# Attention turned by a product, 16-bit integer quantising, and GpSimd on two of eight blocks

## What is computed

```python
# attention, per head: s_mat = scores * d_mat (decay, causal)
h = (s_mat @ v) / (max(abs(sum(s_mat)), exp(-m)) + 5e-5)
h = h * rsqrt(mean(h * h) + 1e-6) * (1 + outnorm_w)
x = x + tanh(g_xattn[0]) * h
# feed-forward: xq = clip(round(x / scale) + zp, -128, 127), scale and zp from min and max of all x
h = gelu(((xq(x) - zx) @ wq(W1).T) * (sx * sw) + b1)          # 128 -> 512
x = x + tanh(g_ffn[0]) * (((xq(h) - zh) @ wq(W2).T) * (sh * sw2) + b2)
```

## Time and profile before

| | |
|---|---|
| median of 3 runs | 905.29 us (905.22 to 906.47) |
| profiled execution: own time | 905.67 us |
| its span | 903.9 us |
| busy: TensorE, VectorE, ScalarE, GpSimd | 617.6, 676.0, 430.6, 196.3 us |
| chain that ended last | TensorE 55%, VectorE 33%, issue 5%, ScalarE 5% |

### The profile page before, as it was taken

How to read it: one execution, slowest core, us unless ns; L and a number is a source line. 1 busy time by engine, 2 the same in 40 slices (tenths; PEclk the granted TensorE clock), 3 DMA queues, 4 the chain that set the end, 5 groups by cost and what they waited for, 6 DMA issues and landing times.

```text
span 903.9 us, 16672 instructions
## 1 busy us (share of the span) xinstructions
PE 617.6 (68%) x5953; PEld 437.7 (48%) x6037; DVE 676.0 (75%) x1896; ACT 430.6 (48%) x892; POOL 196.3 (22%) x160
## 2 busy tenths in 40 slices
PE   4957999923425830000170479999999999999998
PEld 3943444411124630000160376777666777777776
DVE  6658467788979659899799875655666778878775
ACT  2425455457762363333560436556554445445543
POOL 3000168611436002221000036777000000000000
PEclk9999999975555985555585758999999999999999
DMA  7000000000001000000040000000000000001000
GB/s 195 24 1 0 2 1 1 2 1 1 1 14 33 1 1 1 9 12 12 14 140 0 1 1 1 2 2 1 1 2 13 2 13 0 12 0 35 0 13 13
DMA packets 20747, 13.12 MB, mean 15 GB/s; under 512 B 1580, under 2 KB 19240, under 8 KB 20680
## 3 DMA queue, kind: packets, MB, share of 16 engines
q1 hardware_dynamic: 20680, 12.27, 4.9%
HBM read 9.12 MB, written 2.10 MB: 12 GB/s over the span
## 4 chain that ended last, share of the span: by engine, by line
PE 55%; DVE 33%; issue 5%; ACT 5%; SPq 1%; DMA 1%; DVEq 0%; POOL 0%; ACTq 0%; POOLq 0%
PE PS L1494 7%; PE PS L1509 6%; PE PS L1511 6%; PE PS L1510 6%; PE PS L1495 6%; DVE Bm L1078 5%; DVE rowm L1090 5%; PE PS L1493 5%; DVE A L1073 4%; PE PS L1268 2%; PE PS L1334 2%; DVE hmm L1015 2%; DVE hmm L1016 2%; DVE A L728 2%; PE PS L1344 2%
## 5 line engine op out<-in xcount | busy, mean ns | idle before, releaser
L691 ACT ACTIVATE A<-PS,small_t 128x512 f32<-128x512 f32 x256 | 168.4, 688 | 123.9 <-PE PS L1495 122.4
L1509 PE MATMUL PS<-kT_w,A 128*128 128x128 bf16 x1024 | 174.8, 219 | 0.0
L1510 PE MATMUL PS<-kT_w,A 128*128 128x128 bf16 x1024 | 174.8, 219 | 0.0
L1511 PE MATMUL PS<-kT_w,A 128*128 128x128 bf16 x1024 | 174.7, 219 | 0.0
L1184 DVE TENSOR_TENSOR A<-A 128x512 bf16<-128x512 f32 x192 | 123.5, 690 | 12.0 <-ACT A L691 10.8
L1446 PE MATMUL PS<-identf,slab 128*128 128x128 f32 x128 | 21.1, 321 | 125.2 <-ACT xn_w L658 121.8
L1509 PEld LDWEIGHTS PS<-kT_w,A 128*128 128x128 bf16 x1024 | 100.2, 98 | 11.3 <-issue 4.6
L1510 PEld LDWEIGHTS PS<-kT_w,A 128*128 128x128 bf16 x1024 | 100.2, 98 | 6.6
L1494 PE MATMUL PS<-A,xn_w 128*128 128x512 bf16 (+1 forms) x256 | 98.2, 384 | 3.6 <-issue 0.4
L1511 PEld LDWEIGHTS PS<-kT_w,A 128*128 128x128 bf16 x1024 | 100.2, 98 | 0.0
L1495 PE MATMUL PS<-A,xn_w 128*128 128x512 bf16 (+1 forms) x256 | 98.3, 384 | 0.0
(11 more groups left out here) (287 smaller groups left out, 1279.1 us busy)
## 6 DMA issues: line engine op xcount, KB each, us to landing
slab<-in_L_ffn_w_dram SPq DMA_DIRECT2D x16, 256.0 KB, 3.1
xs<-in_x_dram SPq DMA_DIRECT2D x4, 512.0 KB, 6.3
cs<-in_ctx_dram SPq DMA_DIRECT2D x4, 512.0 KB, 6.8
out_dram<-xs SPq DMA_DIRECT2D x8, 256.0 KB, 2.3
A<-Bm SPq DMA_DIRECT2D x9, 64.0 KB, 2.0
xn_w<-in_L_ffn_W_dram SPq DMA_DIRECT2D x2, 256.0 KB, 2.9
A<-Bm SPq DMA_DIRECT2D x4, 36.0 KB, 1.8
A<-Bm SPq DMA_DIRECT2D x4, 24.0 KB, 1.8
```

Of the source, the lines that this page charges most:

```text
L691: act.activation(hf[:, e % 2, c, :], bank(c), ACT.Gelu_apprx_tanh, bias=b1).then_inc(S["h_gelu"], 1)
L1509: pe.matmul(o, hh[:, e % 2, c, t], w2h[:, e, c, :], start=(c == 0 and k == 0), stop=False, skip_group_check=True)
L1510: pe.matmul(o, hh[:, e % 2, c, t], w2l[:, e, c, :], start=False, stop=False, skip_group_check=True)
L1511: ins = pe.matmul(o, hl[:, e % 2, c, t], w2h[:, e, c, :], start=False, stop=(c == NC - 1), skip_group_check=True)
```

## The change

- `turn` is a real f32 product with a constant `tmat` (68 columns of the identity and 64 columns of identity times gain, per half: 132 columns) in place of the transpose. `keep` copies 264 columns, and the gain product of GpSimd (L424) and of `late_norm` (L964) is gone. `tmat` is made on GpSimd once the gain is there, and TensorE waits for it (`turn_made`) ahead of the loop. `oall` is a ring of 16 blocks.
- ScalarE's `keep(b - 2)` stands behind `keep_turned(b - 1)`; `squares`, `divisors` and `mean_squares` come one block earlier; `turn(30)` stands ahead of `weigh(31)`; `ln_stats(1, 0)` is done at block 24. Behind the loop VectorE's order is now `x_range(5, 0)`, `late_norm(6)`, `ln_scales(1, 0)`, `divisors(7)`, `x_range(5, 1)`, `mean_squares(7)`, `x_stats(6)`, `late_norm(7)`, `x_stats(7)`, `x_range(6, 0)`, `ln_stats(1, 1)`, `x_range(6, 1)`, `x_range(7, 0)`, `x_range(7, 1)`.
- Quantising: ScalarE writes int16 with no constant added, VectorE clips int16 to bf16, GpSimd's step is gone. The first 512 columns of x are scaled and clipped by VectorE alone (`xq_first`). The load of the gelu table is asked for ahead of the scaling (`gwarm`).
- Second layer: ScalarE scales six blocks, GpSimd blocks 2 and 5 (`HPOOL`); the clip of nb stands ahead of `add2(nb - 2)` and `x3_stats(nb - 3)`.
- The product of b2 with its gate moves from behind `affine` to ahead of the attention loop.

```diff
+XCUTS = [(512, 1024), (1024, 2048), (2048, 3072), (3072, 4096)]
+HPOOL = [2, 5]
...
-        oall = Bm[:, 4352:8704].rearrange("p (b w) -> p b w", b=B)
+        oall = Bm[:, 4352:8576].rearrange("p (n w) -> p n w", n=16)
+        tmat = Bm[:, 10240:10504].rearrange("p (s c) -> p s c", s=2)
...
+        hqi = Bm[:, 0:8192].bitcast(I16).rearrange("p (c t) -> p c t", c=NC)
+        xqi = Bm[:, 8192:10240].bitcast(I16)
...
+        gwarm = mm[:, 23:24]
...
+            ident4 = identf[:].rearrange("p (j w) -> p j w", j=4)
+            for half in range(2):
+                pool.tensor_copy(tmat[:, half, 0:4 * VW].rearrange("p (j w) -> p j w", j=4), ident4[:, :, 0:VW])
...
             pool.wait_ge(S["gain_ready"], 1)
+            for half in range(2):
+                ins = pool.tensor_tensor(tmat[:, half, 4 * VW:4 * VW + 4 * DH].rearrange("p (j w) -> p j w", j=4), ident4[:, :, 0:DH],
+                                         onw_b[:, 64 * half:64 * half + 64].rearrange("p (j w) -> p j w", j=4), ALU.mult)
+            ins.then_inc(S["turn_made"], 1)
+            pool.wait_ge(S["turn_made"], 1)
...
             def normed(m):
-                chain(pool.tensor_tensor(t.rearrange("p (m w) -> p m w", w=DH), heads(m)[:, :, 0:DH], last(f, DH), ALU.mult), m, 3)
+                chain(pool.tensor_tensor(by_head(osq[:, m % 2]), gained(m), spread_out(f), ALU.mult), m, 3)
...
             def onto(m):
-                t4 = four(osq[:, m % 2])
-                chain(pool.tensor_tensor(t4, t4, rep(onw_b[:], 4), ALU.mult), m, 4)
-                pool.tensor_tensor(g4(xs, m), g4(xs, m), t4, ALU.add).then_inc(S["x2_ready"], 1)
+                pool.tensor_tensor(g4(xs, m), g4(xs, m), four(osq[:, m % 2]), ALU.add).then_inc(S["x2_ready"], 1)
...
             pool.wait_ge(S["scale_ready"], 2)
-            for c in range(4):
-                w = slice(1024 * c, 1024 * c + 1024)
-                pool.wait_ge(S["x_cut"], c + 1)
-                pool.tensor_scalar(xq[:, w], xn_w1[:, w], 1.0, -MAGIC, ALU.mult, ALU.add).then_inc(S["xq_ready"], 1)
...
-            for nb in range(G4):
+            pool.wait_ge(S["scale_ready"], 3)
+            for nb in HPOOL:
...
-                pool.wait_ge(S["h_cut"], nb + 1)
-                pool.tensor_scalar(hq[:, :, w], hid[:, :, w], 1.0, -MAGIC, ALU.mult, ALU.add).then_inc(S["hq_ready"], 1)
+                pool.tensor_scalar(hqi[:, :, w], hid[:, :, w], qs[:, 16:17], 0.0, ALU.mult, ALU.add).then_inc(S["h_pooled"], 1)
...
             def keep(b):
-                own = bank(7, 0, 2 * P).rearrange("p (j w) -> p j w", j=NH)[:, :, 0:VW]
-                act.activation(oall[:, b, :].rearrange("p (j w) -> p j w", j=NH), own, ACT.Copy).then_inc(S["o_kept"], 1)
+                if b % 4 == 0 and b >= 16:
+                    act.wait_ge(S["x2_ready"], b // 4 - 3)
+                act.activation(oall[:, b % 16, :], bank(7, 0, 264), ACT.Copy).then_inc(S["o_kept"], 1)
...
                 weights_exp(b, 0)
-                if b >= 2:
-                    keep(b - 2)
...
-                if b % 4 == 2 and b >= 6:
+                if b >= 2:
+                    keep(b - 2)
+                if b % 4 == 1 and b >= 5:
...
-            roots(G4 - 1)
...
             for b in range(16):
-                if b == 10:
+                if b == 1:
+                    roots(G4 - 1)
+                if b == 12:
...
+            act.activation(gwarm, cst[:, 0:1], ACT.Gelu)
...
             def scale_x(c):
-                v = xn[:, 8 * c:8 * c + 8]
-                act.activation(v, v, ACT.Identity, scale=qs[:, 8:9], bias=cst[:, 2:3]).then_inc(S["x_scaled"], 1)
+                w = slice(*XCUTS[c])
+                act.activation(xqi[:, w], xn_w1[:, w], ACT.Copy, scale=qs[:, 8:9]).then_inc(S["x_scaled"], 1)
...
             act.wait_ge(S["scale_ready"], 3)
-            for nb in range(G4):
-                v = hid[:, :, 512 * nb:512 * nb + 512]
-                act.activation(v, v, ACT.Identity, scale=qs[:, 16:17], bias=cst[:, 2:3]).then_inc(S["h_scaled"], 1)
+            for nb in [n for n in range(G4) if n not in HPOOL]:
+                w = slice(512 * nb, 512 * nb + 512)
+                act.activation(hqi[:, :, w], hid[:, :, w], ACT.Copy, scale=qs[:, 16:17]).then_inc(S["h_scaled"], 1)
...
+            dve.tensor_tensor(ab2_b[:], ab2_b[:], tg[:, 2:3].to_broadcast([P, D]), ALU.mult)
...
-                    x_range(g - 3, 0)
+                    ins = x_range(g - 3, 0)
+                if b == 24:
+                    link(ins)
+                    ln_stats(1, 0)
+                if b % 4 == 1 and g >= 1:
+                    divisors(g - 1)
...
-                    divisors(g - 1)
-                if b % 4 == 3 and g >= 1:
...
             def late_norm(m):
-                link(dve.tensor_tensor(th, heads(m)[:, :, 0:DH], last(f, DH), ALU.mult))
-                link(dve.tensor_tensor(four(t), four(t), rep(onw_b[:], 4), ALU.mult))
+                link(dve.tensor_tensor(by_head(t), gained(m), spread_out(f), ALU.mult))
...
             m = G4 - 1
-            ln_stats(1, 0)
...
-            x_range(m - 2, 1)
+            late_norm(m - 1)
...
-            late_norm(m - 1)
...
-            x_stats(m - 1)
+            x_range(m - 2, 1)
...
-            x_range(m - 1, 0)
-            x_range(m - 1, 1)
+            x_stats(m - 1)
...
-            link(x_range(m, 0))
+            link(x_range(m - 1, 0))
...
+            x_range(m - 1, 1)
+            x_range(m, 0)
...
-            link(dve.tensor_tensor(qs[:, 12:13], qs[:, affine_x + 1:affine_x + 2], qs[:, 0:1], ALU.mult))
-            dve.tensor_tensor(ab2_b[:], ab2_b[:], tg[:, 2:3].to_broadcast([P, D]), ALU.mult).then_inc(S["scale_ready"], 1)
-            ln_apply(1, xs, xn, range(1, 2))
+            dve.tensor_tensor(qs[:, 12:13], qs[:, affine_x + 1:affine_x + 2], qs[:, 0:1], ALU.mult).then_inc(S["scale_ready"], 1)
+            first = xn_w1[:, 0:512]
+            dve.wait_ge(S["ln_half"], 1)
+            link(ts(xqi[:, 0:512], first, qs[:, affine_x:affine_x + 1], None, ALU.mult))
+            ts(xq[:, 0:512], xqi[:, 0:512], qs[:, affine_x + 2:affine_x + 3], qs[:, affine_x + 3:affine_x + 4],
+               ALU.max, ALU.min).then_inc(S["xq_first"], 1)
...
             def cut_x(c):
-                ts(v, v, qs[:, affine_x + 2:affine_x + 3], qs[:, affine_x + 3:affine_x + 4], ALU.max, ALU.min).then_inc(S["x_cut"], 1)
+                ts(xq[:, w], xqi[:, w], qs[:, affine_x + 2:affine_x + 3], qs[:, affine_x + 3:affine_x + 4],
+                   ALU.max, ALU.min).then_inc(S["xq_ready"], 1)
...
-            ln_apply(1, xs, xn, range(2, 3))
+            ln_apply(1, xs, xn, range(1, 3))
...
             for nb in range(G4):
-                v = hid[:, :, 512 * nb:512 * nb + 512]
-                dve.wait_ge(S["h_scaled"], nb + 1)
-                ts(v, v, qs[:, affine_h + 2:affine_h + 3], qs[:, affine_h + 3:affine_h + 4], ALU.max, ALU.min).then_inc(S["h_cut"], 1)
+                w = slice(512 * nb, 512 * nb + 512)
+                if nb in HPOOL:
+                    dve.wait_ge(S["h_pooled"], HPOOL.index(nb) + 1)
+                else:
+                    dve.wait_ge(S["h_scaled"], nb + 1 - sum(n < nb for n in HPOOL))
+                ts(hq[:, :, w], hqi[:, :, w], qs[:, affine_h + 2:affine_h + 3], qs[:, affine_h + 3:affine_h + 4],
+                   ALU.max, ALU.min).then_inc(S["hq_ready"], 1)
+                if nb >= 2:
+                    add2(nb - 2)
...
-                    add2(nb - 3)
-                if nb >= 4:
-                    ins = x3_stats(nb - 4)
+                    ins = x3_stats(nb - 3)
...
-            for nb in range(G4 - 3, G4):
+            for nb in range(G4 - 2, G4):
...
+            pe.wait_ge(S["turn_made"], 1)
...
             def turn(b):
-                    ins = pe.transpose(bank(7, P * half, P * half + P), ot[:, b % 2, half, :], identf[:])
+                    ins = pe.matmul(bank(7, 132 * half, 132 * half + 132), ot[:, b % 2, half, :], tmat[:, half, :], start=True, stop=True)
...
-            weigh(B - 1)
...
+            weigh(B - 1)
...
-                pe.wait_ge(S["xq_ready"], nb // 2 + 1)
+                if nb == 0:
+                    pe.wait_ge(S["xq_first"], 1)
+                else:
+                    pe.wait_ge(S["xq_ready"], nb // 2 + 1)
```

More of the change, by code:

```diff
@@ L7 @@
 BF16 = mybir.dt.bfloat16
+I16 = mybir.dt.int16
 I32 = mybir.dt.int32
@@ L206, in program @@
             "q_masked", "q_summed", "out_cleared", "ld_ready", "sc_ready", "exp_done", "prod_done", "av_done", "ot_kept", "o_turned", "o_kept",
-            "gain_ready", "norm_step", "onto_step", "osq_done", "osum_done", "osqrt_done", "x2_ready",
-            "mm_ready", "mm_turned", "mm_global", "mm_spread", "scale_ready", "x_scaled", "x_cut", "xq_ready",
+            "gain_ready", "turn_made", "norm_step", "onto_step", "osq_done", "osum_done", "osqrt_done", "x2_ready",
+            "mm_ready", "mm_turned", "mm_global", "mm_spread", "scale_ready", "x_scaled", "xq_first", "xq_ready",
```

(27 more changed lines are left out.)

9 lines of the change are left out of this document (4 added, 5 removed).

## The result

The changed kernel takes 893.51 us (median of 4 runs, 891.29 to 894.05) against 905.88 for the kernel before in the same series (905.22 to 906.51). The ratio is 0.9859, 95% interval 0.9839 to 0.9879: 12.4 us faster. The profiled execution took 891.29 us, span 889.4, and is the fastest of the four.

What follows compares the result with a forecast made beforehand. Bounds taken: TensorE waiting for ScalarE's exponential behind `keep` in the attention loop, VectorE behind it and in both layers. Terms +1.2, -3.8, -3.95, -3.2, +2.6, -9.2 sum to -16.35: 905.67 to 889.3 profiled, 888.9 median; range 881 to 897.

Steps and rivals of the forecast that it cites:

- Start of the loop: Ahead of the attention loop: TensorE waits for the turning matrix made on GpSimd, +1.2 us, bounds 0 and 2.
- Loop: Attention loop: the exponential no longer waits for the turn, TensorE's work sets a block of 3.13 us, -3.8 us.
- Behind the loop: VectorE's work after the attention loop: earlier last product, two gain products and one `ln_stats` gone, waits closing, -3.95 us.
- Quantising: Quantising x up to the first maximum: earlier copy, table load hidden in ScalarE's idle time, -3.2 us.
- First layer: First feed-forward layer: a clip meeting GpSimd's sum of b2 is locked out, a new wait, +2.6 us, bounds 0 and 3.
- The rival without a lock: Both layers: GpSimd's sum and scalings run beside the clips, 2.6 and about 1.5 us less, 884.8 us; chance 0.10.
- Second layer: Second feed-forward layer: VectorE's round falls to 2.03 us, last `add2` 21.9 behind the scale, before 31.1; -9.2 us.
- The clause on the memsets: Second layer: GpSimd's memsets, the other row of the queue, cost up to 1 us.
- Four passes a product: Turn in the attention loop: four passes per f32 product, 3.59 us a block, kernel 902.2 us; chance 0.03.
- Turn dear: Turn in the attention loop: at 0.19 us a pass it costs 3.2, kernel 895.9; chance 0.12 for 892.7 to 896.
- GpSimd slow in int16: Second layer: GpSimd's int16 scaling at ten times the price, 19 us a block, kernel 915 us; chance 0.03.
- The rival on 16-bit clips: Second layer: the 16-bit clip is not faster, kernel 892.4 us (chance 0.06) or 899.7 us (chance 0.04).

Runs made afterwards that it cites:

- best2: Against the changed kernel: transposes, no turning matrix, GpSimd's b2 sum behind the clips, 28 keep-warm products, small sums in block 26, GpSimd scaling only block 2: 880.06 us.
- best3: As best2, with VectorE's two steps on the divisors of a group made one block later, ahead of its mean squares: 879.32 us, ratio 0.9703.
- the late sum: Changed kernel with GpSimd's sum of b2 onto the residual waiting until VectorE has made the first layer's four later clips: 889.97 us, ratio 0.9817.

## Why the prediction was right, and where it was off

The time, 893.5, lies in the stated range of 881 to 897, just above the inner one of 885 to 893, and 4.6 above the forecast; the gain was 12.4 of 16.35. Of the missing 4, the distances show 1.9 (14.5 gained in the span); the rest is the gap between the profiled execution and the median.

*Start of the loop* (+1.2 forecast, +2.34): the wait was right (1.3). The step left out what a longer pause does to the granted clock, although the row with the idle 2.96 was on the table. In other traces the whole step is up to +3.1.

*Loop* (-3.8, -2.87): "TensorE's own work sets the block" held, and 3.15 stands against 3.13. The size was off in one term, the turn: four records cost 0.56, 0.14 each, not 0.46 + 0.06; the rest of the block is 2.59, not 2.61. That is 0.4 us over the loop. The other 0.58 is the moved `ln_stats`: "block 24, where VectorE has over 1.5 us free" counted free time on VectorE and did not ask what GpSimd does then.

*Behind the loop* (-3.95, measured -3.81): the sum is right, and partly by luck. The order of `keep` gave 0.91 and not 1.07, and the two gain products 1.07 and not 1.46, so the terms that no run took out must hold more than forecast.

*Quantising* (-3.2, -3.28): the copy starts 1.67 behind the scale (202.33 to 204.00; forecast 1.75), and 4.09 go from it to the first maximum (forecast 4.1). These are rows; no run took a part of this change out.

*First layer* (+2.6, +2.75): the lock is shown by moving the sum: 0.54 against 3.82 for one clip. By the Trainium skill (SBUF - State Buffer, Who interferes with whom), GpSimd and a VectorE instruction in a two-port mode lock each other out for the whole instruction. The traces agree for the clips, 3.82 and 2.42 us long; which mode the small steps ran in, no row shows, but steps on 16 and 32 columns were held too, also by a memset. Not every VectorE instruction is: the maxima (2.29) were not. The rival without a lock falls.

*Second layer* (-9.2, -8.90): the round is 2.16, not 2.03, since the 16-bit clip takes 0.72 and not 0.65. The first clip ended 4.53 behind the scaling, forecast 4.55. "If TensorE's clock rose to 2.4 GHz here, 1 more" had the wrong sign: in the changed kernel it did rise for the middle blocks (a block took 1.05), and VectorE's rounds stayed at 2.16; where the last block ran at full clock too, GpSimd's memset came earlier and cost 1.1. The clause on the memsets, "up to 1", named the right thing, though in the changed kernel they cost nothing. That the clip, the new order and the small sums freed of GpSimd's subtraction (2.4) make up the 8.90 is read from the two timelines: no run takes one of them out, so their shares stay open.

*Four passes a product* (3.59 a block) falls as a price: it is 3.15. *Turn dear*: 0.14 a record is between the two prices I had, 0.111 and 0.19, nearer the cheap one, and the block of 3.37 did not come. *GpSimd slow in int16*: 1.96 a block, against 1.90 for bf16. The rival on 16-bit clips falls too.

Beyond these steps, I did not ask whether the product was worth its place: it was costed against GpSimd's lost work, "costs nothing", when GpSimd had the time and the new order made TensorE the bound.

The median lies 2.2 above the profiled time, which was the first and fastest of its series in both series of this kernel. The start of the span moves by up to 2.2 us between traces, as much as this gap. In other kernels the profiled execution was the slowest of its series (`best2`, `best3`, the late sum), so that it is the fastest here may be chance; it stays open.

Not tried: GpSimd's memsets held back until VectorE's small sums of the third normalisation are over. By the rows it is worth 1.1 us where TensorE is at full clock there.
